# Layer 1's first scores ahead of the last expert's products, its last results and sums behind the maxima, value products ahead of the attention's output products, token sums and low parts placed anew

## What is computed

```python
def _L1_cond_ref(context_c, time_cond, ...):
    full_agg = context_c.mean(axis=1)                      # token sums
    ...
    for e in range(E):
        h = jax.nn.gelu(context_c @ ew1[e] + eb1[e], approximate=True)
        y = h @ ew2[e] + eb2[e]
        out = out + w_be[:, e][:, None, None] * mask[e][None, :, None] * y
    shared = jax.nn.gelu(context_c @ sw1 + sb1, approximate=True) @ sw2 + sb2
    return out + shared

def _attention(x, Wq, bq, Wk, bk, Wv, bv, gamma, beta):
    Q = jax.nn.relu(x @ Wq + bq)
    K = jax.nn.relu(x @ Wk + bk)
    V = jax.nn.relu(x @ Wv + bv)
    scores = jnp.einsum('bqhd,bkhd->bhqk', Qh, Kh) / np.sqrt(dh)
    ...
    attn = jax.nn.softmax(scores, axis=-1)
    out = jnp.einsum('bhqk,bkhd->bqhd', attn, Vh).reshape(B, T, U)
    out = out + x
```

## Time and profile before

| | us |
|---|---|
| median of 3 runs | 1023.08 |
| lowest, highest | 1020.0, 1023.97 |
| profiled execution, its own time | 1024.28 |
| its span, first to last instruction | 1023.0 |
| PE busy | 981.1 (96%) |
| DVE busy | 878.1 (86%) |
| ACT busy | 832.7 (81%) |
| POOL busy | 468.8 (46%) |
| mean granted clock of TensorE | 0.992 |

### The profile page before, as it was taken

How to read it: one execution, slowest core, us unless ns; L and a number is a source line. 1 busy time by engine, 2 the same in 40 slices (tenths; PEclk the granted TensorE clock), 3 DMA queues, 4 the chain that set the end, 5 groups by cost and what they waited for, 6 DMA issues and landing times.

```text
span 1023.0 us, 25958 instructions
## 1 busy us (share of the span) xinstructions
PE 981.1 (96%) x8939; PEld 792.0 (77%) x8939; DVE 878.1 (86%) x3720; ACT 832.7 (81%) x2232; POOL 468.8 (46%) x539
## 2 busy tenths in 40 slices
PE   7999999999999999999989999999989999999897
PEld 7898888988888889733268988888777777776566
DVE  6777989898989898799898899888988888896985
ACT  6888888888888888887787887876778888886786
POOL 2334545454545453506800102101878888893041
PEclk9999999999999999999999999999999999999899
DMA  9000000000000000000000000000000000000002
GB/s 375 32 2 2 2 2 2 2 2 2 2 2 2 2 2 2 2 1 1 0 1 1 1 1 1 1 11 11 23 23 23 23 23 23 23 3 1 1 2 83
DMA packets 8723, 18.31 MB, mean 18 GB/s; under 512 B 1296, under 2 KB 5648, under 8 KB 8208
## 3 DMA queue, kind: packets, MB, share of 16 engines
q1 hardware_dynamic: 8592, 16.65, 4.9%
HBM read 10.36 MB, written 2.10 MB: 12 GB/s over the span
## 4 chain that ended last, share of the span: by engine, by line
PE 79%; DVE 9%; ACT 7%; POOL 3%; issue 2%; DMA 0%; DVEq 0%; ACTq 0%; POOLq 0%
PE PB L245 8%; PE PB L246 8%; PE PB L247 8%; PE PB L341 6%; PE PB L396 6%; PE PB L379 6%; PE PB L1791 5%; PE PB L1763 3%; PE PB L1191 3%; PE PB L1193 3%; PE PB L1192 3%; PE PB L1808 3%; PE PB L428 2%; PE PB L429 1%; PE PB L430 1%
## 5 line engine op out<-in xcount | busy, mean ns | idle before, releaser
L371 POOL TENSOR_TENSOR W<-W,small 128x512 f32<-128x512 f32 x128 | 138.6, 1083 | 217.0 <-DVE small L365 217.0
L360 ACT ACTIVATE W<-W,small 128x128 f32<-128x128 f32 x512 | 198.8, 390 | 29.5 <-DVE small L351 28.9
L245 PE MATMUL PB<-RR_s 128*128 128x256 f32 (+3 forms) x568 | 185.5, 327 | 5.9 <-DVE RR_s L1143 2.5
L246 PE MATMUL PB<-RR_s 128*128 128x256 f32 (+3 forms) x568 | 177.4, 312 | 0.0
L247 PE MATMUL PB<-RR_s 128*128 128x256 f32 (+3 forms) x568 | 177.4, 312 | 0.0
L351 DVE CUSTOM_DVE_ANT_0 W<-PB,W 128x128 f32<-128x128 f32 x512 | 117.2, 284 | 39.9 <-PE PB L341 38.8
L1779 POOL TENSOR_TENSOR AR_s<-AR_s,small 128x512 f32<-128x512 f32 x128 | 129.5, 1042 | 29.2 <-DVE small L1772 29.1
L1165 ACT ACTIVATE AR_s<-PB,W 128x512 f32<-128x512 f32 (+2 forms) x160 | 100.6, 630 | 30.1 <-PE PB L247 24.7
L245 PEld LDWEIGHTS PB<-RR_s 128*128 128x128 f32 x568 | 109.3, 192 | 14.0 <-issue 4.4
L1179 DVE TENSOR_TENSOR RR_s<-AR_s,RR_s 128x512 fp32r<-128x512 f32 (+2 forms) x160 | 99.8, 633 | 17.9 <-ACT RR_s L1170 14.4
L1772 DVE CUSTOM_DVE_ANT_0 AR_s<-PB,W 128x128 f32<-128x128 f32 x512 | 110.9, 286 | 2.8 <-PE PB L1763 0.5
(11 more groups left out here) (384 smaller groups left out, 2441.3 us busy)
## 6 DMA issues: line engine op xcount, KB each, us to landing
W<-in_w SPq DMA_DIRECT2D x1, 5809.5 KB, 25.1
W<-in_w SPq DMA_DIRECT2D x2, 1024.0 KB, 7.3
out<-XT SPq DMA_DIRECT2D x8, 256.0 KB, 2.3
XF<-in_xT SPq DMA_DIRECT2D x3, 512.0 KB, 10.4
W<-AR_s SPq DMA_DIRECT2D x16, 64.0 KB, 2.1
AR_s<-AR_s SPq DMA_DIRECT2D x16, 64.0 KB, 2.1
QS<-AR_s SPq DMA_DIRECT2D x12, 64.0 KB, 2.1
KR<-AR_s SPq DMA_DIRECT2D x12, 64.0 KB, 2.1
```

What stands on the lines that cost most here:

```text
L245: nc.tensor.matmul(out, lh, rh, start=True, stop=False)
L246: nc.tensor.matmul(out, ll, rh, start=False, stop=False)
L360: e = nc.scalar.activation(SS[r][:, hl], SS[r][:, hl], ACTF.Exp, bias=mx[r][:, h:h + 1], scale=-1.0, accum_out=rc[r][:, h:h + 1])
L371: nc.gpsimd.tensor_tensor(s3, s3, over(rc[r], 2, [128, 4, 128]), ALU.mult).then_inc(s_nrm, 1)
```

## The change

All edits are in the order of work and in the place of tiles; nothing that is computed changes.

- The sums of chunks 2 and 3 move from job 0's last quarter to step t = 17 of the coupling network, on both sides of `dve_part(0)`.
- The low parts of chunks 1 and 2 move from DVE to POOL (`pool_part`), behind POOL's last step of the coupling network.
- PE makes only quarter 0 of the last job's second products ahead of the scores of sequence 0, and quarters 1 to 3 behind them.
- DVE makes the results of the last two jobs behind the first 16 maxima, and their sums in q = 1, behind the next 16 maxima and the masks; its own wait for the last sum falls away.
- ACT waits for the last sum before its first `act_o5`; `OT5` now lies on the columns of `YT`, and `VT`, `VY`, `SS5` and `PT5` lie 1024 columns further on. POOL's code in the attention is as it was.
- `pe_v5(q + 1)` stands ahead of `pe_PV5(q - 2)` instead of behind it and behind query and key; the plan of the banks says the same.

```diff
@@ -824,7 +824,7 @@
         FIRST_TURN = (1, 2, 3, 4)
-        AGG = {16: [(0, 0), (0, 1)], 22: [(1, 0), (1, 1)], 23: [(2, 0), (2, 1)], 24: [(3, 0), (3, 1)]}
+        AGG = {16: [(0, 0), (0, 1)], 23: [(2, 0), (2, 1)], 24: [(3, 0), (3, 1)]}
@@ -1141,6 +1141,11 @@
                 dve.wait_ge(s_up, 4 * last_job(c - 3) + 4)
             dve.wait_ge(s_xh, c + 1)
             nc.vector.tensor_tensor(XL[c % 3], cs(XF, c), XH[c % 3], ALU.subtract).then_inc(s_xl, 1)
+
+        def pool_part(c):
+            pool.wait_ge(s_xl, c)
+            pool.wait_ge(s_xh, c + 1)
+            nc.gpsimd.tensor_tensor(XL[c % 3], cs(XF, c), XH[c % 3], ALU.subtract).then_inc(s_xl, 1)
         def pe_up(n, k):
             c, x = JOBS[n]
@@ -1430,7 +1435,7 @@
                         pe_keysum(0, PB[7])
                     if n < NJ:
                         pe_up(n, k)
-                    if n and 4 * n + k < 4 * NJ + 3:
+                    if n and 4 * n + k <= 4 * NJ:
                         pe_down(n - 1, k)
                     if (n, k) in GATING_MM:
                         pe_gating(GATING_MM[(n, k)])
@@ -1516,8 +1521,9 @@
             dve_adapt(4)
             for t in range(5, 19):
                 if t == 17:
+                    dve_agg(1, 0)
                     dve_part(0)
-                    dve_part(1)
+                    dve_agg(1, 1)
                 for p in range(4):
                     for a in AGG.get(t, ()):
                         if a[0] == p:
@@ -1530,7 +1536,7 @@
                         if p_ == p and (p, y, st) != (3, 2, 4):
                             dve_couple(p, y, st)
             for n in range(NJ + 1):
-                for c in parts_before(n):
+                for c in parts_before(n) if n > 1 else ():
                     dve_part(c)
                 for k in range(4):
                     if AHEAD.get((n, k)) == 2:
@@ -1539,11 +1545,11 @@
                         dve_up(n, k)
                     if n == 0 and k:
                         dve_couple(3, 2, 4, [(0,), (2,), (3,)][k - 1])
-                    if n > 1 and k == 0:
+                    if 1 < n < NJ and k == 0:
                         dve_add(n - 2)
                     for a in AGG.get(19 + 4 * n + k, ()):
                         dve_agg(*a)
-                    if n and n < NJ:
+                    if n and 4 * n + k < 4 * NJ - 1:
                         dve_down(n - 1, k)
                     if (n, k) in GATING:
                         dve_gating(GATING[(n, k)])
@@ -1561,6 +1567,8 @@
                     pool_couple(p, y, st)
                 if t < 14:
                     pool_split(t - 4)
+            pool_part(1)
+            pool_part(2)
             for i in range(7):
                 pool_gating(i)
             for job, tile in ((10, QS[0][:, :]), (13, KR[0][:, :]), (16, QS[1])):
@@ -1605,11 +1613,11 @@
         scratch("s5", 22720)
         QT, KT = ar(512), ar(512)
         X2 = [ar(512) for _ in range(2)]
+        OT5 = [ar(512) for _ in range(2)]
         VT = [ar(128) for _ in range(2)]
         VY = [ar(512) for _ in range(3)]
         SS5 = [ar(512) for _ in range(6)]
         PT5 = [ar(512) for _ in range(8)]
-        OT5 = [ar(512) for _ in range(2)]
         XA = ar(256).rearrange("p (b r) -> p b r", r=8)
         KR[1] = ar(2048)
         XBP = [ar(128) for _ in range(2)]
@@ -1711,11 +1719,11 @@
                 plan_T5(4 * q - 4)
                 plan_T5(4 * q - 3)
                 plan_asides(q, TURNED)
+                if q + 1 < NB5:
+                    passes5(("v", q + 1), 6, s_vt, q + 2)
                 if q >= 2:
                     passes5(("o", q - 2), 4, s_o5, q - 1)
                 plan_asides(q, PROJECTED)
-                if q + 1 < NB5:
-                    passes5(("v", q + 1), 6, s_vt, q + 2)
                 plan_asides(q, MULTIPLIED)
                 plan_T5(4 * q - 2)
                 plan_T5(4 * q - 1)
@@ -2556,7 +2564,8 @@
         def pe_attend2():
             pe.wait_ge(s_ge, 4 * NJ)
             pe_S5(0)
-            pe_down(NJ - 1, 3)
+            for k in (1, 2, 3):
+                pe_down(NJ - 1, k)
             pe.wait_ge(s_qt, 1)
             pe.wait_ge(s_kt, 1)
             pe.wait_ge(s_kx, 1)
@@ -2576,11 +2585,11 @@
                     pe_T5(4 * q - 4)
                     pe_T5(4 * q - 3)
                 steps_of(turned, q)
+                if q + 1 < NB5:
+                    pe_v5(q + 1)
                 if q >= 2:
                     pe_PV5(q - 2)
                 steps_of(projected, q)
-                if q + 1 < NB5:
-                    pe_v5(q + 1)
                 steps_of(multiplied, q)
                 if q:
                     pe_T5(4 * q - 2)
@@ -2622,6 +2631,8 @@
                 step_of(beside, 4 * q)
                 step_of(beside, 4 * q + 1)
                 act_exp5(4 * q)
+                if q == 2:
+                    act.wait_ge(s_pa, added(NJ - 1))
                 if q >= 2:
                     act_o5(q - 2)
                 step_of(beside, 4 * q + 2)
@@ -2654,9 +2665,8 @@
             dve.wait_ge(s_kd[0], spreads(0))
             for u in range(4):
                 dve_max5(u)
+            dve_down(NJ - 2, 3)
             dve_down(NJ - 1, 3)
-            dve_add(NJ - 1)
-            dve.wait_ge(s_pa, added(NJ - 1))
             dve_v5(0)
             beside = {"keysum": dve_keysum5, "masks": dve_masks5, "factors": dve_factors, "mean": dve_mean, "b1": dve_b1,
                       "gamma": dve_gamma5, "select": dve_select5, "add": dve_add5}
@@ -2672,6 +2682,8 @@
                     dve_max5(4 * q + 3)
                 if q == 1:
                     dve_masks5(0)
+                    dve_add(NJ - 2)
+                    dve_add(NJ - 1)
                 step_of(beside, 4 * q + 1)
                 if q + 1 < NB5:
                     dve_v5(q + 1)
```

## The result

| us | before | after |
|---|---|---|
| median of 20 runs each, taken in turn | 1023.19 | 1025.25 |
| lowest, highest | 1019.62, 1024.97 | 1022.77, 1027.38 |
| profiled execution, its own time | 1024.28 | 1023.15 |
| its span | 1023.0 | 1021.9 |
| mean granted clock | 0.992 | 0.995 |

The ratio after to before is 1.0021, with a 95% interval of 1.0011 to 1.0030: some 2.1 us slower, well inside the 0.5% that I took as no change. The forecast was 1024.1, and no change.

A forecast was written before the change was run, and what follows sets the result against it. PE was taken to bound the kernel, with 79% of the chain that ends last. Terms -1.8 + 3.2 + 1.2 - 1.6 = +1.0 us against the median gave 1024.1, range 1019 to 1028, forecast as no change.

The forecast's parts named there:

- part 2: Handover: first scores ahead of three quarters of the last job's products start earlier; -1.2 us taken alone, swallowed by the hold.
- part 3: Handover: last sums behind maxima and masks hold POOL's clearing of VY, delaying PE's transpose 2; +3.2 us, bounds -1.2 to +3.8.
- Part 1: First expert jobs: low parts on POOL and earlier sums remove PE's 2.26 us idle stretch; -1.8 us, bounds 0 to -3.7.
- Part 4: Handover: PE's idle stretch of 4.6 us brings the lower clock behind it; +1.2 us, bounds 0 to +1.8.
- Part 5: Attention: value products ahead of PV fill PE's waits, five q's lose 0.25 each; -1.6 us, bounds -5.1 to +1.3.
- first rival: Handover: POOL's wait delays nothing PE needs, parts 3 and 4 together become -1.2; total -4.6 us, 1018.5; chance 0.17.
- slower rival: Attention: early value products delay ACT's chain in all 28 q's; +7.0 instead of -1.6, total +9.6, 1032.7; chance 0.08.

The follow-up runs named there:

- e1: Kernel before with only the first-jobs edits (token sums moved, low parts of chunks 1 and 2 on POOL): 1020.92 against 1022.12, ratio 0.9982.
- e2: Kernel before with only the handover edits (scores ahead of three quarters, results and sums later, tiles reordered): 1027.97 against 1022.12, ratio 1.0051.
- e9: Version after with the low part of chunk 2 given back from POOL to DVE: 1025.1 against 1022.89 for the kernel before, ratio 1.0017.
- e3: Kernel before with only the value product moved ahead of PV: 1022.0 against 1022.12, ratio 0.9998; attention 191.91 us in the trace.
- e4: Version after without POOL's wait for the last sum ahead of clearing VY: 1018.37 against 1022.12 for the kernel before, ratio 0.9961.
- e5: Version after with four unused products added in PE's idle stretch at the handover: 1022.23 against 1022.68 for the kernel before, ratio 1.0002.
- e10: e4 with the value product ahead of PV only where no tokens or gamma precede it: 1017.54 against 1022.89 for the kernel before, ratio 0.9944.
- e6: Version after with the two last sums between sequence 1's second and third set of maxima: 1020.92 against 1022.68 for the kernel before, ratio 0.9988.

## Why the prediction was right

The forecast sum was +1.0, measured +1.85 between the two traces and +2.1 between medians. Term by term, part 2 being held in part 3:

| part | forecast | measured | from |
|---|---|---|---|
| 1 first jobs | -1.8 | -1.67 | landmarks, e1 |
| 3 POOL's hold, part 2's gain in it | +3.2 | +3.0 | transpose 2: 16.59 - 13.57 |
| 4 clock | +1.2 | +2.3 | rest of the handover: (26.88 - 16.59) - (21.57 - 13.57); 1.8 in e2, 1.5 in e9 |
| 5 values | -1.6 | -1.8 | landmarks, e3 |

*Part 1.* Right in size and in kind: no long idle stretch, no low clock. The low clock was less of it than the sum implied: with the old order at full clock (e2, e3) the gain is 1.45. DVE's rounding beside POOL lost 0.55, not 0.35, since POOL's own instruction began 0.15 later behind job 0's first product than I had laid it and took 1.30 instead of 1.09. The rule cited from the Trainium skill (SBUF — State Buffer, "SBUF: two separate sides"), that a two-input DVE operation and a GpSimd one take the shared port pair in turn, agrees with the trace: the row of 1.23 and e9's 0.68 are its two sides, and the roundings that meet no POOL instruction are at 0.68. The overlap was longer than the loss, though: 0.69 against 0.55 here, 0.89 against 0.75 at the sum L1221 before, and no run shows why. What the meeting cost in the end is bounded by e9: at most the 0.60 of pitch that DVE was spared.

*Part 2.* The first scores came at +0.79 and the second at +5.85 behind the last gelu (forecast 0.8 and 5.7), the first exponential, held by the tokens' copy and the table load, at 6.70 (6.69). The gain was swallowed by the hold after, as forecast; in e4 it is there: 1.46 against the profile before, of which some 0.3 is that profile's slow scores (1.1 and 1.3 against e1 and e3); forecast 1.2.

*Part 3.* The chain stood as laid out, counted from the last gelu: clearing at 12.84 (forecast 12.97), exponential 4 at 15.33 (15.45), transpose 2 at 16.59 (16.7). e4 shows that POOL's wait is the cause: without it transpose 2 comes at 12.10. Against the old order at full clock (12.91) the hold is +3.7, and against the slow scores of the profile before, on which the sum was made, +3.0. It also shows that the first rival (the hold is covered) was wrong about what happens, but right about what an unheld handover is worth: e4 took 3.75 us less than before, where that rival gave 4.6.

*Part 4* is the term that was mis-sized. I took +1.2, with an upper bound of +1.8, from low stretches of 3 and 3.6 us behind idle times of 2.26 and 1.11. Behind 4.33 us PE worked at the low clock from 723.86 to about 728.7, 4.9 us, and e5 takes out 2.07 of the loss by filling the idle time. It is not one number: behind idle times of 4.11 (e2) and 4.33 (e9) PE worked slowly for some 3.4 and 3.1 us only, and the term is 1.8 and 1.5. All three lie above what I took, one above my bound. The bound halved the longest stretch that a row showed; the forecast idle time was twice as long as that of any row, and the bound should have been left open upwards. That the sum landed within 1.1 us all the same is due to the other terms, each right to 0.2.

*Part 5.* Saved waits and new waits both as forecast. The new wait costs 0.22 (forecast 0.25) at five q's, as e10 shows by removing it. A cycle of four sequences went from 26.72 to 26.50 us, 0.22 instead of my 0.14, which makes up the 0.2 in the sum. The slower rival (the value product delays ACT's chain in every q) is out: only the five q's with gamma and query show it.

What stays open: why e3's 1.83 us of the trace are not seen in full in its runs, and why the same wait keeps the clock in one execution and not in another.

## What to carry over

When work is moved back on one engine, list every wait on the other engines that is counted on it, in the lines that the diff leaves alone above all, and read what is queued behind such a wait: here one wait on a side engine turned a gain of 1.5 us into a loss of 5.3. When a move also changes the layout, ask of each old wait whether its reason is still there; e4 is a one-line deletion worth 6.8 us in the traces. Of an idle stretch on the matrix engine count the clock beside the time: here 3.0 us of hold brought 1.5 to 2.3 us of loss by slow products, of which e5 got 2.1 back with products whose results nobody reads.

## What the runs showed of the hardware that I had not expected

- Idle time on TensorE does not decide the clock by its length alone. An idle time of 1.11 us ahead of the second scores was followed by scores of 1.89 us in the profile before, and by this in e1, with the same code there:

```profile
713.13 1.17 PE L1771 MATMUL PB<-KR,QS 32*128 32x128 f32 x32 [1.11 <-DVE small L1780]
```

  Likewise 1.90 us in the version after and in e9, above, and 2.26 us before against 2.25 in e2 and e3. Behind 4.1 and 4.3 us (e2, after, e9) the clock was low each time, behind 0.90 and 1.64 (e5, e6) it stayed up. Nor does the fall stand at a fixed place: in the version after the clock is 0.50 from 722 on, with PE idle until 723.86, while in e2 it is still 1.00 from 727.0 to 727.5, behind PE's start at 727.09, and 0.50 from 728. A kernel with such waits has two prices for them, here 0.2 us apart in the first jobs (19.90 before, 19.68 in e2), 0.4 us at the second scores (handover 21.57 before, 21.21 in e1) and 1.6 us at the transposes (attention 193.52 in e9, 191.92 after).
- POOL's subtraction took 1.28 and 1.30 us in the first jobs instead of 1.09, whatever DVE did beside it: in e9, where POOL makes only the first of the two and no rounding of DVE meets it, it is 1.28 too. Why this line (L1148) is slower than L1093 no run shows.
